# Attention row sums: a packed V matrix, with exponentials added up by DMAs, GpSimd and VectorE

## What is computed

```python
scores = jnp.einsum('bhsd,btd->bhst', Q, Kc) * scale
attn = jax.nn.softmax(scores, axis=-1)
out = jnp.einsum('bhst,btd->bhsd', attn, Vc)
out = out.transpose(0, 2, 1, 3).reshape(B, S, d) @ Wo.T
X = X + out
```

## Time and profile before

| | us |
|---|---|
| median of 3 runs | 1461.44 (1456.23 to 1464.70) |
| the profiled execution | 1461.01 |
| its span in the trace | 1459.0 |
| PE busy | 1307.4 (90%) |
| DVE busy | 1079.0 (74%) |
| ACT busy | 893.1 (61%) |
| POOL busy | 385.4 (26%) |

### The profile page before, as it was taken

The page is one execution under the profiler, slowest core; times in us unless marked ns, Lnnn a source line. Parts: engine busy times, 40 slices in busy tenths (PEclk is TensorE's granted clock), DMA queues, the critical chain, the costliest instruction groups (busy, mean ns, idle before and its releaser), DMA issues.

```text
span 1459.0 us, 19334 instructions
## 1 busy us (share of the span) xinstructions
PE 1307.4 (90%) x6008; PEld 920.7 (63%) x6008; DVE 1079.0 (74%) x2143; ACT 893.1 (61%) x1450; POOL 385.4 (26%) x282
## 2 busy tenths in 40 slices
PE   4777677999999999999998999999997999999994
PEld 2334545665666665676665666666664797887774
DVE  4956987777887777777885877787974867546778
ACT  2355564776766766666686766666675856555551
POOL 0443431222311212211111311111154001623346
PEclk9989797999999999999999999999998999999998
DMA  5001016200000000000000001000011323555634
GB/s 196 1 1 44 15 58 208 81 1 1 1 1 1 1 1 1 1 1 1 1 1 1 1 1 44 1 0 1 22 51 65 104 93 117 195 148 165 191 115 149
DMA packets 56418, 75.82 MB, mean 52 GB/s; under 512 B 8383, under 2 KB 48063, under 8 KB 56064
## 3 DMA queue, kind: packets, MB, share of 16 engines
q1 hardware_dynamic: 36030, 46.29, 9.7%
q0 software_dynamic: 6144, 16.79, 3.7%
q10 hardware_dynamic: 14146, 11.52, 2.3%
HBM read 37.27 MB, written 37.22 MB: 51 GB/s over the span
## 4 chain that ended last, share of the span: by engine, by line
PE 63%; DVE 19%; issue 5%; ACT 5%; POOL 5%; DMA 1%; ACTq 1%; POOLq 0%; DVEq 0%; SPq 0%
PE PS L1802 8%; PE PS L1700 6%; PE PS L1749 6%; PE PS L1732 6%; PE PS L1751 6%; PE PS L1735 6%; PE PS L1750 6%; DVE mx L1159 5%; PE PS L1828 4%; DVE PL L1189 4%; PE PS L1713 3%; POOL y L1534 2%; PE PS L1686 2%; POOL xbuf L1522 2%; PE PS L1786 1%
## 5 line engine op out<-in xcount | busy, mean ns | idle before, releaser
L1159 DVE TENSOR_REDUCE mx<-PS 128x1 f32<-128x512 f32 x512 | 344.1, 686 | 100.6 <-PE PS L1700 98.5
L770 ACT ACTIVATE PT<-PS 128x1024 f32<-128x1024 f32 x256 | 262.8, 1027 | 231.8 <-PE PS L1735 221.8
L1514 POOL TENSOR_TENSOR PL<-PT,PH 128x1024 fp32r<-128x1024 f32 x61 | 146.2, 2396 | 541.8 <-ACT PH L775 530.1
L775 ACT ACTIVATE PH<-PT 128x1024 fp32r<-128x1024 f32 x256 | 271.2, 1060 | 8.1
L1189 DVE TENSOR_TENSOR PL<-PT,PH 128x1024 fp32r<-128x1024 f32 x195 | 238.9, 1225 | 44.4 <-ACT PH L775 43.8
L1749 PE MATMUL PS<-PH,VH 128*65 128x512 f32 x512 | 219.6, 429 | 8.6 <-DVE PL L1189 8.6
L1751 PE MATMUL PS<-PL,VH 128*65 128x512 f32 x512 | 202.9, 396 | 0.0
L1750 PE MATMUL PS<-PH,VL 128*65 128x512 f32 x512 | 202.3, 395 | 0.0
L1700 PE MATMUL PS<-KA,Q 128*128 128x512 f32 x384 | 161.1, 432 | 16.9 <-DVE mx L1159 12.1
L1732 PE MATMUL PS<-Q,KA 128*128 128x512 f32 x384 | 128.0, 415 | 2.5 <-POOL KB L1491 2.5
L1735 PE MATMUL PS<-Q,KB 65*128 65x512 f32 x384 | 122.6, 401 | 0.0
(11 more groups left out here) (239 smaller groups left out, 2486.5 us busy)
## 6 DMA issues: line engine op xcount, KB each, us to landing
xbuf<-xT SPq DMA_DIRECT2D x26, 384.0 KB, 4.4
xg<-xbuf SPq DMA_DIRECT2D x78, 128.0 KB, 2.3
ybuf<-yo ACTq DMA_DIRECT2D x78, 128.0 KB
nxT<-in_wexp SPq DMA_DIRECT2D x9, 768.0 KB, 4.4
x<-in_x SPq DMA_DIRECT2D x8, 512.0 KB, 11.9
x_scratch<-x SPq DMA_DIRECT2D x2, 2048.0 KB, 6.9
nxT<-x_scratch SPq DMA_DIRECT2D x32, 128.0 KB
out<-X SPq DMA_DIRECT2D x32, 128.0 KB, 1.9
```

Source lines behind the costliest of these rows:

```text
L770: act.activation(PT[:, gs % 2, :], PS[:, bk:bk + 2, :].rearrange("p a n -> p (a n)"), ACT.Exp, scale=0.125).then_inc(sem("pt"), 1)
L775: act.activation(PH[:, gs % 3, :], PT[:, gs % 2, :], ACT.Copy).then_inc(sem("pt_h"), 1)
L1159: dve.tensor_reduce(mx[:, half, i, c:c + 1], PS[:, k, :], AX, ALU.max).then_inc(sem("dve_out"), 1)
L1514: pool.tensor_tensor(PL[:, gs % 3, :], PT[:, gs % 2, :], phf[:, gs % 3, :], ALU.subtract).then_inc(sem("pl_g"), 1)
```

## The change

V is packed: `V` is 128 wide, high part in columns 0 to 63 and low part in 64 to 127, and one matmul by PH gives both. The second matmul, high V by PL, writes to the first 64 output partitions alone. The column of ones is gone. `O` is now 128 by 1024, for one query half, and `woa` has the output weights twice, once for the high rows and once for the low ones, so that `proj` adds the two.

Z is now computed beside. PT, the fp32 exponentials, has three buffers, and every step's PT is added into a sum over the group:
- key tiles 0 and 1: SyncE writes PT (512 KB) to DRAM, `zbuf[g, 0]` and `zbuf[g, 1]`;
- tiles 2 to 7, 9, 11, 13, 15: GpSimd issues a DMA that adds PT to one of the two by turns. Each waits for the one before it on the same sum, on GpSimd's queue;
- tiles 8, 10, 12, 14: GpSimd itself copies (8) or adds PT into `Z`, after `low` of that step;
- in steps 1 and 3 of the next group, `collect`: two DMAs, one after the other, add the two DRAM sums to `Z`;
- in step 6 of the next group `z_mm`: eight fp32 matmuls of Z by a column of ones, 1024 sums, and one reciprocal of 128 by 8 on VectorE, where there was one in each `proj`.

`exp(gs)` now waits for `low(gs - 3)` and for the adding of step gs - 3 to be complete (`summed`). The last group (g = 15) is summed by VectorE, one operation in each step, behind `low`. `low` is VectorE's in all 256 steps, with two buffers of PL. `proj` of a block's first half moves into that block (steps 22 to 31), that of the second half to steps 6 to 15 of the next, and only eight are left for the tail.

The diff, cut to its core (renamed operands, waits at the end, and lists of jobs are left out):

```diff
-POOL_EVERY = 4
+ZPOOL = (8, 10, 12, 14)
+ZDMA = [kc for kc in range(16) if kc not in ZPOOL]
...
+        todo += [(66, ("z_mm", bh, 0))] + spread(proj_jobs(bh, 0), 68, 93)
         if bh > 0:
-            m, e = (30, 60) if bh == 4 else (49, 92)
-            todo += spread(proj_jobs(bh - 1)[:8], 4, m) + spread(proj_jobs(bh - 1)[8:], m + 1, e)
+            todo += [(18, ("z_mm", bh - 1, 1))] + spread(proj_jobs(bh - 1, 1), 20, 46)
...
-    last = [x for j, p in enumerate(proj_jobs(7)) for x in (p, norm[j])] + [norm[NT]]
+    proj = proj_jobs(7, 1)
+    last = norm[:8] + [("z_mm", 7, 1)] + proj + norm[8:]
...
-def by_pool(gs):
-    return gs % POOL_EVERY == POOL_EVERY - 1 and gs < 7 * NSTEP + 20
...
+    zbuf = nc.dram_tensor("z_scratch", [15, 2, P, 1024], F32, kind="Internal").ap()
...
-    VH = sb("VH", [P, NB * NT, 65], F32R, c=c3)
-    VL = sb("VL", [P, NB * NT, 65], F32R, c=c3)
+    V = sb("V", [P, NB * NT, 2, 64], F32R, c=c3)
...
-    rz = sb("rz", [P, 2, 1], c=c3)
+    rz = sb("rz", [P, 2, 8], c=c3)
+    ones = sb("ones", [P, 1], c=c3)
...
+    with ExitStack() as c:
+        ZL = sb("ZL", [P, 1024], c=c)
...
-    PT = sb("PT", [P, 2, 1024], c=c3)
+    PT = sb("PT", [P, 3, 1024], c=c3)
     PH = sb("PH", [P, 3, 1024], F32R, c=c3)
-    PL = sb("PL", [P, 3, 1024], F32R, c=c3)
-    O = sb("O", [65, S], c=c3)
-    woa = sb("woa", [65, 4, 257], c=c3)
+    PL = sb("PL", [P, 2, 1024], F32R, c=c3)
+    Z = sb("Z", [P, 1024], c=c3)
+    O = sb("O", [P, 1024], c=c3)
+    woa = sb("woa", [P, 4, D], c=c3)
...
+    def summed(w, gs):
+        g, kc = divmod(gs, 16)
+        if g == 15:
+            w.wait_ge(sem("zv"), kc + 1)
+        elif kc in ZPOOL:
+            w.wait_ge(sem("zp"), 4 * g + ZPOOL.index(kc) + 1)
+        else:
+            n, c = divmod(ZDMA.index(kc), 2)
+            if n == 0:
+                w.wait_ge(sem(f"d_zw{c}"), 16 * (g + 1))
+            else:
+                w.wait_ge(sem(f"d_za{c}"), 16 * (5 * g + n))
...
+        def total(gs):
+            g, kc = divmod(gs, 16)
+            if g < 15 and kc < 2:
+                w.wait_ge(sem("pt"), gs + 1)
+                sp.dma_start(zbuf[g, kc], PT[:, gs % 3, :]).then_inc(sem(f"d_zw{kc}"), 16)
...
-        sp.dma_start(woa[:, :, :], I["woA"]).then_inc(sem("d_woa"), 16)
+        for a in (0, 64):
+            sp.dma_start(woa[a:a + 64, :, :], I["woA"][0:64, :, 0:D]).then_inc(sem("d_woa"), 16)
         w.wait_ge(sem("zero"), 1)
         for b in range(NB):
             zv = xbuf[b].rearrange("(n p a) d -> n p a d", p=P, a=3)
             for n in range(NTI // 3):
                 sp.dma_start(zv[n], bc(zero, 3, 1)).then_inc(sem("d_zero"), 16)
         for gs in range(NGS):
...
-            if gs >= 2:
-                low_done(w, gs - 2)
-            act.activation(PT[:, gs % 2, :], PS[:, bk:bk + 2, :].rearrange("p a n -> p (a n)"), ACT.Exp,
+            if gs >= 3:
+                w.wait_ge(sem("pl"), gs - 2)
+                summed(w, gs - 3)
+            act.activation(PT[:, gs % 3, :], PS[:, bk:bk + 2, :].rearrange("p a n -> p (a n)"), ACT.Exp,
                            scale=0.125).then_inc(sem("pt"), 1)
             w.wait_ge(sem("pt"), gs + 1)
             if gs >= 3:
                 w.wait_ge(sem("av"), 2 * (gs - 2))
-            act.activation(PH[:, gs % 3, :], PT[:, gs % 2, :], ACT.Copy).then_inc(sem("pt_h"), 1)
+            act.activation(PH[:, gs % 3, :], PT[:, gs % 3, :], ACT.Copy).then_inc(sem("pt_h"), 1)
         def o_out(gs, n):
             bh, i = divmod(gs, NSTEP)
             qc, kc = divmod(i, 16)
             if kc < 15:
...
-            q0 = qc * 1024 + n * 512
             w.wait_ge(sem("av"), 2 * gs + n + 1)
-            if bh:
-                pe_of(w, ("proj", bh - 1, 8 * qc + 7, 0))
-            act.activation(O[:, q0:q0 + 512], PS[0:65, 4 + n, :], ACT.Copy).then_inc(sem("o"), 1)
+            if qc:
+                pe_of(w, ("proj", bh, 7, 0))
+            elif bh:
+                pe_of(w, ("proj", bh - 1, 15, 0))
+            act.activation(O[:, n * 512:n * 512 + 512], PS[:, 4 + n, :], ACT.Copy).then_inc(sem("o"), 1)
...
+        def total(gs):
+            g, kc = divmod(gs, 16)
+            if g < 15:
+                return
+            q_free(w, 8)
+            if kc == 0:
+                dve.tensor_copy(ZL[:, :], PT[:, gs % 3, :]).then_inc(sem("zv"), 1)
+            else:
+                w.wait_ge(sem("zv"), kc)
+                dve.tensor_tensor(ZL[:, :], ZL[:, :], PT[:, gs % 3, :], ALU.add).then_inc(sem("zv"), 1)
+        def z_mm(bh, qc):
+            k = banks.bank["z_mm", bh, qc, 0]
+            pe_of(w, ("z_mm", bh, qc, 0))
+            if bh:
+                out_of(w, ("proj", bh - 1, 8 * qc + 7, 0))
+            dve.reciprocal(rz[:, qc, :], PS[:, k, 0:8]).then_inc(sem("dve_out"), 1)
         def proj(bh, i):
-            b, s, k = bh // 4, i % 2, banks.bank["proj", bh, i, 0]
-            n = b * NT + i
+            b, k = bh // 4, banks.bank["proj", bh, i, 0]
+            n, qc = b * NT + i, i // 8
             pe_of(w, ("proj", bh, i, 0))
-            mark(dve.reciprocal(rz[:, s, :], PS[:, k, 256:257]))
-            w.wait_ge(own, made[0])
+            out_of(w, ("z_mm", bh, qc, 0))
             if bh % 4:
                 out_of(w, ("proj", bh - 1, i, 0))
-            dve.scalar_tensor_tensor(X2[:, n, :], PS[:, k, 0:256], rz[:, s, :], X2[:, n, :], ALU.mult,
+            dve.scalar_tensor_tensor(X2[:, n, :], PS[:, k, 0:256], rz[:, qc, i % 8:i % 8 + 1], X2[:, n, :], ALU.mult,
                                      ALU.add).then_inc(sem("dve_out"), 1)
         def low(gs):
             w.wait_ge(sem("pt_h"), gs + 1)
             if gs == 0:
                 front_done(w)
-            if gs >= 3:
-                w.wait_ge(sem("av"), 2 * (gs - 2))
-            dve.tensor_tensor(PL[:, gs % 3, :], PT[:, gs % 2, :], phf[:, gs % 3, :], ALU.subtract).then_inc(sem("pl_v"), 1)
+            if gs >= 2:
+                w.wait_ge(sem("av"), 2 * (gs - 1))
+            dve.tensor_tensor(PL[:, gs % 2, :], PT[:, gs % 3, :], phf[:, gs % 3, :], ALU.subtract).then_inc(sem("pl"), 1)
...
-            if not by_pool(gs):
-                low(gs)
+            low(gs)
+            total(gs)
             for part in range(3):
...
-        def low(gs):
-            w.wait_ge(sem("pt_h"), gs + 1)
-            if gs >= 3:
-                w.wait_ge(sem("av"), 2 * (gs - 2))
-            after_last("pl_g")
-            pool.tensor_tensor(PL[:, gs % 3, :], PT[:, gs % 2, :], phf[:, gs % 3, :], ALU.subtract).then_inc(sem("pl_g"), 1)
+        def total(gs):
+            g, kc = divmod(gs, 16)
+            if g == 15:
+                return
+            if kc in ZPOOL:
+                w.wait_ge(sem("pl"), gs + 1)
+                after_last("zp")
+                if kc == ZPOOL[0]:
+                    if g:
+                        pe_of(w, ("z_mm", *divmod(g - 1, 2), 0))
+                    pool.tensor_copy(Z[:, :], PT[:, gs % 3, :]).then_inc(sem("zp"), 1)
+                else:
+                    pool.tensor_tensor(Z[:, :], Z[:, :], PT[:, gs % 3, :], ALU.add).then_inc(sem("zp"), 1)
+            elif kc >= 2:
+                n, c = divmod(ZDMA.index(kc), 2)
+                w.wait_ge(sem("pt"), gs + 1)
+                summed(w, 16 * g + ZDMA[2 * n - 2 + c])
+                pool.dma_start(zbuf[g, c], PT[:, gs % 3, :], accum_op=ALU.add).then_inc(sem(f"d_za{c}"), 16)
+        def collect(g, c):
+            summed(w, 16 * g + ZDMA[10 + c])
+            summed(w, 16 * g + ZPOOL[3])
+            if c:
+                w.wait_ge(sem("d_z"), 16 * (2 * g + 1))
+            pool.dma_start(Z[:, :], zbuf[g, c], accum_op=ALU.add).then_inc(sem("d_z"), 16)
...
-            if by_pool(gs):
-                low(gs)
+            total(gs)
+            if gs >= 16 and gs % 16 in (1, 3):
+                collect(gs // 16 - 1, gs % 16 // 2)
...
+            w.wait_ge(sem("d_woa"), 32)
+            q0 = n * P
             w.wait_ge(sem("o"), 4 * bh + 2 * qc + n // 4 + 1)
             k = bank("proj", bh, i, 0)
-            pe.matmul(PS[:, k, 0:257], O[0:65, i * P:i * P + P], woa[0:65, bh % 4, :], start=True,
+            pe.matmul(PS[:, k, 0:D], O[:, q0:q0 + P], woa[:, bh % 4, :], start=True,
                       stop=True).then_inc(sem("pe_use"), 1)
+        def z_mm(bh, qc):
+            g = 2 * bh + qc
+            w.wait_ge(sem("ones"), 1)
+            if g < 15:
+                w.wait_ge(sem("d_z"), 32 * (g + 1))
+            else:
+                w.wait_ge(sem("zv"), 16)
+            k, z = bank("z_mm", bh, qc, 0), Z[:, :] if g < 15 else ZL[:, :]
+            for i in range(8):
+                mm = pe.matmul(PS[:, k, i:i + 1], z[:, i * P:i * P + P], ones[:, :], start=True, stop=True)
+            mm.then_inc(sem("pe_use"), 1)
...
-            low_done(w, gs)
+            w.wait_ge(sem("pl"), gs + 1)
             out_of(w, ("v_mm", b, kc // 4, 0))
             if kc == 0 and gs:
                 w.wait_ge(sem("o"), 4 * bh + 2 * qc + n - 1)
```

(11 more changed lines are left out.)

38 lines of the change are left out of this document (14 added, 24 removed), and 2 rows, old and new, of the table READERS.

## The result

The changed kernel takes 1537.45 us (median of 4 runs, 1534.92 to 1545.4); the kernel before, run beside it on the same chip, 1460.63 us. The ratio is 1.0529, with a 95% interval of 1.0494 to 1.0564: 5.3% slower, 77 us. That lies 92 us above the forecast of 1445 and 17 above the end of the range. Later runs were on several chips, on which the kernel before took 1461 to 1499 us, so each is told as a ratio to the kernel before on its own chip.

What follows compares the result with a forecast made beforehand. TensorE bounds the kernel before (731 of 770 us in blocks 0 to 6). Forecast: 1461.0 - 19 (blocks 0 to 6) + 6 (block 7) - 3 (tail) = 1445 us; own range 1420 to 1475, 8 in 10 from 1405 to 1520.

Steps and rivals of the forecast that it cites:

- TensorE's work: Blocks 0 to 6: 731 us, less 103.5 for two AV matmuls of six, plus 26 for z_mm, gives 653 us.
- VectorE's work: Blocks 0 to 6: 590.2 us plus 55 (GpSimd's subtractions, fewer reciprocals) gives 645, 665 with locks.
- The surcharge: Stalls on top of the busier engine's work in blocks 0 to 6: 9% taken, bounds 5.3% (700) and 15% (765); 725 us.
- The lock: VectorE's subtractions wait for GpSimd's adds at tiles 10, 12, 14: some 0.5 us, 42 times, +20 us, between 0 and 42.
- The adding DMA: DMA sums in the loop: issue to landing 4.7 us, between 3.5 and 7.0; no cost up to 7.1.
- L: Time of one adding DMA from issue to landing, a link of the chain; forecast 4.7 us, costly from 7.1 on.
- SyncE's queue: Loop start: tile 0's write waits behind 26 zeroing DMAs, delaying exponential 4; +23 us, +26 with 3 of lower clock.
- It cannot be caught up: Loop start: the +26 us of the wait behind the zeroing DMAs stays in the kernel's time.
- z_mm: Blocks 0 to 6, TensorE: 13 times 16 instructions at 2.00 us each, +26 us.
- The clock: After the start's hole of 23 us, 1.2 GHz for some ten matmuls more, 3 us.
- Block 7: First 20 steps 71 us against 65.0, +6, between 0 and 10; last 12 steps GpSimd's; the tail -3.
- adding DMA too slow: Rival: chain of tiles 2, 4, 6 costs from L = 7.1 on; at L = 9, 1520 us; chance 0.2.

Runs made afterwards that it cites:

- no_pool_adds: Changed kernel with GpSimd's three additions per group (tiles 10, 12, 14) left out and its tile 8 copy replaced by an add of 1.0; ratio 1.0280.
- bare: Changed kernel without any sum, the last group's included, and with one matmul of eight in z_mm; ratio 0.9760.
- before_packed: Kernel before with packed V alone: two of six AV matmuls per step gone, the sum Z left out wholly; ratio 0.9653.
- half_low: ones_inside with each subtraction from the fifth on done on 512 of its 1024 columns; ratio 0.9272.
- no_sums: Changed kernel without any sum of groups 0 to 14 (no DMA sums, no GpSimd additions); last group still summed, z_mm kept; ratio 0.9917.
- no_collect: Changed kernel without the two collecting DMAs per group, and GpSimd's tile 8 copy replaced by an add of 1.0; ratio 1.0374.
- plain_writes: Changed kernel with each group's ten adding DMAs as plain writes, waits and order kept, tile 8 copy replaced by an add of 1.0; ratio 1.0297.
- zero_late: Changed kernel with its 26 zeroing DMAs issued one per four steps inside SyncE's loop, not all ahead of it; ratio 1.0434.
- before_packed_low: before_packed with all subtractions on VectorE (61 more of 1.226 us, 75 us), none on GpSimd; ratio 0.9737.
- before_low_on_vector: Kernel before with all subtractions on VectorE (61 more of 1.226 us, 75 us) and nothing else changed; ratio 1.0034.
- ones_inside: Kernel before with V packed as 64 high columns, one of ones and 63 low, so TensorE keeps the sum; ratio 0.9694, 1416 us.

## Why the prediction was wrong

- **TensorE's work** came out: the AV matmuls of packed V start 0.23 us apart at the full clock, as said. (The 2,683 matmuls stand in eight more groups beside L1750's, not six; the sum is right.)
- **VectorE's work** came out to the microsecond, by luck: 665 us forecast with the locks, 90.80 + 573.81 = 664.6 in blocks 0 to 6. Without them it was 634 (no_pool_adds) where 645 had been forecast, and the additions put 30 on it where the forecast had 20. In blocks 1 to 6 it was busy 82% of the time, not over 85%.
- **The surcharge**, "I take 9%", is the first step that failed. bare has 94.2 + 641.5 = 735.7 us in blocks 0 to 6. TensorE's work there, by the forecast's rows, is 731 - 103.5 + 13 x 0.25 = 631; so the surcharge is 17%, above the upper bound of 15%. No sums and no locks are in that.

```profile
235.00:329.20 94.20, 87.58 (x342) 62.11 (x343) 84.47 (x114) 67.50 (x67) 1.40 (x2) 0.95 0.35 115
329.20:970.70 641.50, 587.34 (x2390) 406.40 (x2389) 543.49 (x785) 454.68 (x518) 26.02 (x28) 0.98 0.01 3
```

  The surcharge in before_packed, where VectorE's work is the old 590 us, is 15% already: it has 725 us over 627.5. So most of the surcharge came with TensorE's smaller load, and less with VectorE's larger one. half_low shows that after packing VectorE's time counts too. That both come from the turns of two engines on two banks is argued; no run changes the banks. Without sums (no_sums) the seven blocks took 751, where my 725 was to hold locks as well: 26 us.
- **The lock** was the right mechanism in the right place, mis-sized: +20 on VectorE forecast, +27 in its subtractions alone, 36 us on the kernel. The 1.7 to 2 us forecast for the subtractions after tiles 10, 12 and 14 were 1.48, 2.27 and 1.62. The forecast let its cost vanish within the 9%; it came off the kernel in full.
- **The adding DMA**, "4.7, no cost up to 7.1", failed twice. L is 5.6 in the median and up to 10.1; and the threshold took L as one number with nothing beside it. The collecting DMAs were counted as GpSimd's issues and nothing more; no_collect shows 23 us for them (give or take 10). All DMA sums cost 48, of which the forecast had only the start. The Trainium skill, "DMA: Bandwidth & Descriptors", Anatomy of one DMA — SWDGE (gpsimd) path, gives 2.0 us + bytes/436e3 for a DMA issued by GpSimd, an estimated 3.2 us for 512 KB; plain_writes agrees with 3.0. Adding costs 2.6 us on top here, 5.6 against 3.0.
- **SyncE's queue** came out: exponential 4 at 267.45 (forecast 266), a lower clock after it (PEclk 0.84 in block 0). Block 0 is 38 us longer than before, and 27 of these go with the zeroing in zero_late (forecast 26). "It cannot be caught up" is open: of the 27 only 14 are won back when the zeroing moves (zero_late), but the zeroing then stands in the loop; without any DMA sums block 0 is 31 us shorter, and the other blocks don't give it back.
- **`z_mm`** at 2.00 us each was to cost 26 us; seven eighths of it cost 6 in the changed kernel, and some 18 where nothing hides it (bare, one execution).
- **The clock** in the loop was not in the forecast beyond 3 us at the start. It is 0.96 in blocks 1 to 6, 0.97 in no_sums, 0.98 in bare and 0.99 in before_packed. What that costs no run shows.
- **Block 7**: +13 against +6; the tail +1 against -3. before_packed, with no sum and no more work on VectorE, already has 113 us in the table's last column where 102 stood; why is open.

The misses in blocks 0 to 6 add up to the 82. Of them 26 us lie between the forecast's 725 and no_sums' 751. The other 56 are the sums': they take the stretch from 751 to 833, which happens to be 82 us too, and 26 of that had been forecast for the start. The rival "adding DMA too slow" (1520) was nearest in number, and that is luck: the price was 48 us for all DMA sums, with L under its threshold. What the forecast called -103.5 for TensorE in blocks 0 to 6 was worth 45 us there (770 to 725 in before_packed). The change spent 7.6%, 112 us (1.0529 - 0.9765), on a sum that had been free in column 65.

## What to carry to other kernels

Before work is moved off the busiest engine, ask what the second gets, and price the pair. Here TensorE's work filled 95% of the stretch and VectorE was busy for 77% of it, and a us taken off TensorE gave under half a us (51 for 119). What a us on VectorE is worth hangs on the case and has to be measured: 45 for 79 taken off in half_low (with GpSimd's subtractions halved too), 36 for 27 of lock, but 12 and 5 for 75 put on in before_packed_low and before_low_on_vector, which also freed GpSimd of its slower subtractions. A row that rides in a matmul cost nothing here (ones_inside and before_packed are level in the loop); look for a place to keep it (a spare column) before building a path of DMAs and additions around it. Price a chain of DMAs at its slowest link with everything else that the new code puts on the engines, not at the median of one alone.

## What was not expected of the hardware

An adding DMA of 512 KB from SBUF to DRAM landed in 5.6 us and a plain one in 3.0, in the same place and queue; GpSimd's queue took 40.7% of the 16 engines' time with adding and 22.5% without, for the same 111.17 MB. This is that row of the two pages, the changed kernel first:

```profile
q0 software_dynamic: 32064, 111.17, 40.7%
```

```profile
q0 software_dynamic: 32064, 111.17, 22.5%
```

An adding DMA from DRAM into SBUF was slower still in the median, 9.4 us, and 6.6 beside plain writes; its fastest took 5.6, near the 5.0 of the fastest into DRAM, so most of the difference is what ran beside it. The chips differed where the two kernels are alike: the tail took 346.3 us in ones_inside and 368.2 in before_packed, with the same work. Why isn't known.
